# A pipelined attention kernel: near V in two transfers, regrouped Q/K stacks, a new setup and a new slot order

## What is computed

```python
OFFSETS = sorted(set(range(0, 33)) | {48, 64, 96, 128, 192, 256, 384})
qkv = x @ Wqkv + bqkv                      # q, k, v: 16 heads of 16
scores = [(q * shift(k, d)).sum(-1) * HD**-0.5 + pos_bias for d in OFFSETS]
alpha = softmax(scores)                    # over the offsets, d > position left out
out = sum(alpha[d] * shift(v, d) for d in OFFSETS)
x = layernorm(x + (out * sigmoid(x @ Wgate + bgate)) @ Wout + bout)
ids, probs = top2(relu(x @ rw1 + rb1) @ rw2 + rb2)
y = sum over the two experts of probs * expert(x), at most 1024 tokens an expert
out = layernorm(x + y)
```

## Time and profile before

| what | value |
|---|---|
| three runs, median | 1947.17 us (1945.5 to 1951.18) |
| the profiled execution: its own time, its span | 1936.55 us, 1934.8 us |
| mean granted TensorE clock | 0.761 of full speed |
| busy: TensorE, VectorE, ScalarE, GpSimd | 72%, 52%, 46%, 37% of the span |
| setup | to about 29 us |
| attention, 16 sequences | to about 1460 us |

### The profile page before, as it was taken

How to read it: one execution, slowest core, us unless ns; L and a number is a source line. 1 busy time by engine, 2 the same in 40 slices (tenths; PEclk the granted TensorE clock), 3 DMA queues, 4 the chain that set the end, 5 groups by cost and what they waited for, 6 DMA issues and landing times. The chain is left out here.

```text
span 1934.8 us, 72320 instructions
## 1 busy us (share of the span) xinstructions
PE 1400.3 (72%) x31232; PEld 893.4 (46%) x31232; DVE 1003.3 (52%) x2117; ACT 898.4 (46%) x1544; POOL 715.9 (37%) x654
## 2 busy tenths in 40 slices
PE   2345776877777786777777686877864599999970
PEld 1223444444444444444444444545542267666750
DVE  5214354655555555655655564655664355555425
ACT  3131462634454463635445363645453465566526
POOL 6021322624333352634434352634333122233235
PEclk9665676968676776867667686867676799999995
DMA  4483524436352434536252434535210534444328
GB/s 113 69 232 114 113 69 91 118 83 127 89 121 72 102 83 90 117 76 128 75 111 64 102 84 80 112 77 125 50 48 14 170 63 116 93 89 94 68 32 349
DMA packets 220104, 194.55 MB, mean 101 GB/s; under 512 B 66848, under 2 KB 207152, under 8 KB 219649
## 3 DMA queue, kind: packets, MB, share of 16 engines
q1 hardware_dynamic: 204464, 175.11, 36.5%
q0 software_dynamic: 15360, 15.10, 5.0%
HBM read 98.07 MB, written 86.18 MB: 95 GB/s over the span
## 5 line engine op out<-in xcount | busy, mean ns | idle before, releaser
L396 POOL TENSOR_TENSOR p<-p 128x512 f16<-128x512 f32 x96 | 129.5, 1349 | 357.8 <-ACT p L795 357.6
L809 ACT COPY featT<-gp 128x1024 f16<-128x1024 f16 x96 | 93.4, 1032 | 362.7 <-PE gp L541 362.7
L396 DVE TENSOR_TENSOR p<-p 128x512 f16<-128x512 f32 x96 | 85.5, 891 | 268.5 <-ACT p L795 268.2
L548 PE MATMUL gp<-featT,wr 128*128 128x512 f16 x768 | 191.5, 407 | 21.0 <-DVE mT L958 15.1
L1106 POOL DMA_INDIRECT disp<-y,sidx x128 | 180.1, 1407 | 53.2 <-issue 37.9
L1363 POOL DMA_INDIRECT xln<-y,place x64 | 104.9, 1640 | 217.5 <-DVE y L1505 176.2
L1401 PE MATMUL up<-rowsT,w 128*128 128x512 f16 x768 | 171.3, 383 | 8.7 <-DVE w L1478 5.3
L1415 PE MATMUL dn<-w,h 128*128 128x256 f16 x1536 | 170.1, 273 | 0.0
L1415 PEld LDWEIGHTS dn<-w,h 128*128 128x128 f16 x1536 | 149.7, 98 | 17.3
L794 ACT ACTIVATE p<-st 128x512 f16<-128x512 f32 x192 | 116.7, 608 | 77.9 <-PE st L592 75.1
L1462 ACT ACTIVATE h<-up,b 128x512 f16<-128x512 f32 x128 | 88.3, 690 | 128.7 <-PE up L1401 70.0
(11 more groups left out here) (174 smaller groups left out, 2881.7 us busy)
## 6 DMA issues: line engine op xcount, KB each, us to landing
qk_dram<-qk SPq DMA_DIRECT2D x64, 256.0 KB, 2.5
v_near<-vs SPq DMA_DIRECT2D x224, 66.0 KB
qs<-qk_dram SPq DMA_DIRECT2D x96, 128.0 KB, 4.4
ks<-qk_dram SPq DMA_DIRECT2D x96, 128.0 KB, 7.4
o_dram<-o_far SPq DMA_DIRECT2D x64, 136.0 KB, 7.3
o_back<-o_dram SPq DMA_DIRECT2D x16, 544.0 KB, 4.2
v_dram<-vs SPq DMA_DIRECT2D x16, 528.0 KB
v_far<-v_dram SPq DMA_DIRECT2D x64, 132.0 KB
```

Source lines behind the costliest of these rows:

```text
L396: engine.tensor_tensor(p16[:, b, 1, :], p32[:, b, :], p16[:, b, 0, :], ALU.subtract).then_inc(is_split, 1)
L548: last = nc.tensor.matmul(dst, lhs(a, c), rhs(b, c), start=(k == 0), stop=(k == len(todo) - 1))
L809: gp_done(nc.scalar.copy(featT[:, i, :, :].rearrange("f c t -> f (c t)"), bank[:, :].bitcast(F16)), n, stage, PART_OF_T[stage], i)
```

## The change

Q and K stacks: the columns of the weights and the bias are permuted in the setup so that channel d of the eight heads of one parity lie beside each other. A row of a stack is then one run of 8 KB in DRAM. SP stores the high halves as soon as ScalarE has them (`qk_hi`), reads rows 0 to 15 of each half with four DMAs of 128 KB (`hi_in`), then stores the low halves and reads the other 32 rows with four DMAs of 256 KB (`rest_in`). The maxima wait for the first, the scores for the second.

Near V: `v_near` is read from `v_dram`, which has 32 rows of zeros in front, by two DMAs of 64 rows. `vs` has one buffer. SP waits there, as before, until the near values of the sequence before are done.

Order: the gated transposes (`outp t`) go from slot 5 to slot 4, the first near scores from 4 to 5, the last near values from 15 to 16, the exponential of head half 0 of pair 0 from slot 0 to the slot before, and the subtraction `y` on VectorE two slots later.

Setup: x is loaded in it, `v_far` is cleared by ScalarE, `ks` by two whole memsets, and the first weights are split in smaller pieces. ScalarE issues six of the eight clearings of `disp` there and two at the end of iteration -1. SP regroups the bias through DRAM and writes the two pads of `v_dram`.

```diff
-    3: [("rank", "l"), ("proj", "vg1")], 4: [], 5: [("outp", "t"), ("rank", "c")],
+    3: [("rank", "l"), ("proj", "vg1")], 4: [("outp", "t")], 5: [("rank", "c")],
...
+         ("dve", "outp", "y"): 3,
...
-SCORES_AT = [-1, 0, 4, 7, 10, 12]
-EXP_AT = [0, 1, 5, 8, 11, 13]
+SCORES_AT = [-1, 0, 5, 7, 10, 12]
+EXP_AT = [[-1, 1, 5, 8, 11, 13], [0, 1, 5, 8, 11, 13]]
 SPLIT_AT = [1, 2, 6, 9, 12, 14]
-VALUES_AT = [2, 4, 7, 10, 13, 15]
+VALUES_AT = [2, 4, 7, 10, 13, 16]
...
-    v_dram = [dram(f"v_dram{i}", (N, H * VW), F16) for i in range(2)]
+    v_dram = [dram(f"v_dram{i}", (BLOCK + N, H * VW), F16) for i in range(2)]
...
-    qk_dram = [dram(f"qk_dram{i}", (4, D, N), F16) for i in range(2)]
+    qk_dram = [dram(f"qk_dram{i}", (2, 2, 2, P, N), F16) for i in range(2)]
...
-                if n.i is None and n.c == 0 and 1 <= h <= CLEARINGS:
-
-                    rows = slice((h - 1) * SLOTS // CLEARINGS, h * SLOTS // CLEARINGS)
-                    sync.dma_start(disp[rows, :].rearrange("(b p t) d -> p b (t d)", p=P, t=TILES),
...
                     wait(sp, pv_done, n.at(UNIT_PAIRS))
-                    sp.wait_ge(v_split, n.at(TILES, TILES))
+                    sp.wait_ge(v_stored, n.at(16, 16))
                     for u in range(2):
...
+                        half = PAIRS * VW
+                        src = bass.AP(v_dram[n.par].tensor, half * u, [[2 * half, 2 * BLOCK], [2 * half * BLOCK, N // BLOCK], [1, half]])
+                        dst = v_near[2 * BLOCK * u:2 * BLOCK * (u + 1), :, u, :, :]
+                        sync.dma_start(dst.rearrange("w b h c -> w b (h c)"), src).then_inc(v_near_in, 16)
...
-                sp.wait_ge(qk_split, n.at(4, 2 * w + 2))
                 if w == 0:
-                    wait(sp, stack_in[n.par], n.half(192))
...
+                    wait(sp, hi_in[n.par], n.half(64))
+                    wait(sp, rest_in[n.par], n.half(64))
+                sp.wait_ge(qk_hi, n.at(4, 2 * w + 2))
+                store(n, w, 0, qk_hi_stored)
                 if w == 0:
                     return
-                sp.wait_ge(qk_stored, n.at(64, 64))
                 for e in range(2):
                     wait(sp, st_full[e], n.at(UNIT_PAIRS, -UNIT_PAIRS))
...
+                sp.wait_ge(qk_hi_stored, n.at(32, 32))
+                for w, dst in ((0, qs), (1, ks)):
                     for e in range(2):
...
+                        src = qk_dram[n.par][w, e, PLACE[w][0]].rearrange("(d p) t -> d (p t)", p=PAIRS)
+                        sync.dma_start(dst[n.par][STACK * e:STACK * e + HD, :, :].rearrange("r p t -> r (p t)"), src).then_inc(hi_in[n.par], 16)
+                for w in range(2):
+                    sp.wait_ge(qk_split, n.at(4, 2 * w + 2))
+                    store(n, w, 1, qk_lo_stored)
+                sp.wait_ge(qk_lo_stored, n.at(32, 32))
+                for w, dst in ((0, qs), (1, ks)):
+                    for e in range(2):
+                        src = qk_dram[n.par][w, e].rearrange("i (d p) t -> (i d) (p t)", p=PAIRS)
+                        sync.dma_start(dst[n.par][STACK * e + HD:STACK * e + MROW, :, :].rearrange("r p t -> r (p t)"), src).then_inc(rest_in[n.par], 16)
...
-            load_x(Batch(None, 0))
+            for i in range(2):
+                sync.dma_start(v_dram[i][0:BLOCK, :], v_near_flat[0:BLOCK, 0:H * VW]).then_inc(pad_in, 16)
+            sp.wait_ge(pad_in, 32)
...
                 if k == 0:
+                    alone.wait_ge(rest_in[n.par], n.half(64, 64))
                     alone.wait_ge(m_in[n.par], n.half(32, 32))
...
-                    pe.wait_ge(stack_in[n.par], n.half(192, 192))
+                    pe.wait_ge(hi_in[n.par], n.half(64, 64))
...
-                        nc.scalar.activation(qk16[:, 0, u, :], bank[:, :], ACT.Identity, bias=bqk[:, u:u + 1], scale=scale)
+                        nc.scalar.activation(qk16[:, 0, u, :], bank[:, :], ACT.Identity, bias=bqk[:, u:u + 1], scale=scale).then_inc(qk_hi, 1)
...
+                if it.i is None and it.c == -1 and k == H - 1:
+
+                    act.wait_ge(rest_in[0], 64)
+                    for c in range(CLEARED_IN_SETUP, CLEARINGS):
+                        clear_slots(nc.scalar, disp, y16[0], c).then_inc(cleared, 16)
...
+                act.wait_ge(zeroed, 1)
+                for c in range(CLEARED_IN_SETUP):
+                    clear_slots(nc.scalar, g["disp"], zero_rows, c).then_inc(a["cleared"], 16)
+                wide = a["v_far_flat"][:, :].bitcast(FP32).rearrange("p (b c) -> p b c", c=704)
+                nc.scalar.copy(wide, zero_rows[:, :, :].rearrange("p t d -> p (t d)").bitcast(FP32)[:, 0:704].unsqueeze(1).to_broadcast([P, 6, 704]))
```

More of the change, by code:

```diff
@@ L202, in pair_at, with clear_slots @@
             return it.shift(-(at // H)), k
+def clear_slots(eng, disp, zero_rows, part):
+    rows = slice(part * SLOTS // CLEARINGS, (part + 1) * SLOTS // CLEARINGS)
+    return eng.dma_start(disp[rows, :].rearrange("(b p t) d -> p b (t d)", p=P, t=TILES),
+                         zero_rows[:, :, :].rearrange("p t d -> p (t d)").bitcast(U32).unsqueeze(1).to_broadcast([P, SLOTS // CLEARINGS // P // TILES, TILES * ROW // 2]))
 def tail(rows, dt):
@@ L290, in attention @@
         vg32 = sb("vg32", [P, 2, 2 * D], FP32)
-        vs = [sb(f"vs{i}", [P, TILES, H, VW], F16) for i in range(2)]
+        vs = sb("vs", [P, TILES, H, VW], F16)
         eg = [sb(f"eg{i}", [P, TILES * H, HD], FP32) for i in range(2)]
@@ L609, in values @@
                 if k == FAR_PAIRS:
-                    alone.wait_ge(v_near_in, n.at(256, 256))
+                    alone.wait_ge(v_near_in, n.at(32, 32))
                 p = lambda e, a, c: p16[:, 2 * (k % 2) + e, a, c:c + BLOCK]
@@ L1169, in _ @@
             def _(sp):
-                for k, (dst, src) in enumerate(loads):
-                    sp.dma_start(dst, src, allow_slow_non_contiguous=True).then_inc(here[k] if k < 6 else loaded, 16)
+                for k, (dst, src) in enumerate(loads[0:5]):
+                    sp.dma_start(dst, src, allow_slow_non_contiguous=True).then_inc(here[k], 16)
+                sp.dma_start(a["xin"][:, :, :], g["x_rows"][0:N, :].rearrange("(t p) d -> p t d", p=P)).then_inc(a["x_loaded"], 16)
+                sp.dma_start(*loads[5], allow_slow_non_contiguous=True).then_inc(here[5], 16)
+                for u in range(4):
+                    src = g["bqkv"][D * (u // 2):D * (u // 2 + 1)].rearrange("(p e d) -> e d p", e=2, d=HD)[u % 2]
+                    sp.dma_start(g["bqk_dram"][u].rearrange("(d p) -> d p", p=PAIRS), src, allow_slow_non_contiguous=True).then_inc(regrouped, 16)
+                for dst, src in loads[6:]:
+                    sp.dma_start(dst, src, allow_slow_non_contiguous=True).then_inc(loaded, 16)
+                sp.wait_ge(regrouped, 64)
+                sp.dma_start(a["bqk"][:, :], g["bqk_dram"].rearrange("u f -> f u"), allow_slow_non_contiguous=True).then_inc(loaded, 16)
                 sp.wait_ge(vec_done, 1)
@@ L1186, in _ @@
                     last = nc.gpsimd.memset(t[:, :], 1.0)
-                for i in range(2):
-                    last = nc.gpsimd.memset(a["vs"][i][:, :, :, HD:HD + 1], 1.0)
+                last = nc.gpsimd.memset(a["vs"][:, :, :, HD:HD + 1], 1.0)
                 last.then_inc(base, 1)
@@ L1227, in _ @@
                 for i in range(2):
-                    for e in range(2):
-                        nc.vector.memset(a["ks"][i][STACK * e + 32:STACK * (e + 1), :, :].bitcast(FP32), TWO_ONES)
+                    nc.vector.memset(a["ks"][i][:, :, :].rearrange("p a t -> p (a t)").bitcast(FP32), TWO_ONES)
                 for v in (vec_n[0], vec_f[0]):
@@ L1234, in _, with split @@
                 last.then_inc(vec_base, 1)
+                def split(k):
+                    src, h, l = splits[k]
+                    dve.wait_ge(hi, k + 1)
+                    nc.vector.scalar_tensor_tensor(l, src, WS, h, ALU.mult, ALU.subtract).then_inc(lo, 1)
+                for k in range(11):
+                    split(k)
                 dve.wait_ge(here[5], 16)
@@ L1244, in _ @@
                 last.then_inc(vec_done, 1)
-                for k, (src, h, l) in enumerate(splits):
-                    dve.wait_ge(hi, k + 1)
-                    nc.vector.scalar_tensor_tensor(l, src, WS, h, ALU.mult, ALU.subtract).then_inc(lo, 1)
+                for k in range(11, len(splits)):
+                    split(k)
 def experts(nc, g):
```

95 lines of the change are left out of this document (44 added, 51 removed).

## The result

The changed kernel takes 1864.92 us in the median of four runs (1862.24 to 1871.79), the kernel before 1946.34 us beside it: ratio 0.9608, 95% interval 0.9579 to 0.9637. The forecast was 1785, its range 1745 to 1860. So the sign was right, and half of the gain did not come: 81 us in place of 162.

| stretch | before | after | forecast | measured |
|---|---|---|---|---|
| start to the first mT | 83.9 | 90.5 | -16 | +6.6 |
| first to second mT (iteration 0) | 88.7 | 70.3 | -20 | -18.4 |
| second to last mT (14 periods) | 1197.9 | 1144.2 | -126 | -53.7 |
| last mT to the end of the span | 564.3 | 565.0 | 0 | +0.7 |

What follows compares the result with a forecast made beforehand. TensorE's start of near maximum 2 was taken as set by a chain: second far evacuation, store, landing, read back, merge, reduction. Periods 126, start 16 and iteration 0 20 sum to 162 us: 1774.6 profiled, 1785 median; range 1745 to 1860.

Steps and rivals of the forecast that it cites:

- Second far scores: Exponential of head half 0 moved earlier on ScalarE, so TensorE's wait for it goes: 2.84 us per period.
- High halves: Four stack reads instead of twelve ahead of near maximum 0: operands 13 us sooner, its wait goes entirely.
- Low halves and the rest: Low halves stored behind the first reads, then four 256 KB reads: done at 736.7, not holding the far sums.
- slow rest: Rival: 32-row stack reads go no faster than 16-row ones, done at 740.8; 5.4 us per period, 1835; chance 0.20.
- slower case: Rival: 8 KB runs on few rows make stack reads slower, sign under 90 GB/s; about 2050; chance 0.03.
- Gated transposes: Moved ahead of the first near scores on TensorE: 1.5 us to spare, no new wait; projection's 3.32 us wait goes.
- Late gate: Rival: gated low half on VectorE comes 4.5 us later, 3 lost per period: 42 us, 1827; chance 0.12.
- The chain: Far sums' store, o_back read and merge ahead of near maximum 2: 6.2 us sooner per period, still the next bound.
- Near V: Sixteen issues on SP become two from DRAM, its wait for the last near values covered: nothing added, nothing gained.
- The start: Ahead of the first near maximum: x loaded early 4.15 us, high halves 12 us sooner; sum 16 us.
- long setup: Rival: SP's small setup loads wait 15 us for the six clearings, first maximum gains 1 not 16; 1800; chance 0.10.
- Iteration 0: Clearings between transfers 14 us and an ordinary period's 9 go, less 3 for two clearings left: 20 us.

Runs made afterwards that it cites:

- old_order_y: Changed kernel with the slot tables of the kernel before, but the subtraction y kept at its new place two slots later; 1920.05 us, ratio 0.9894.
- old_order: Changed kernel with the slot tables of the kernel before, y early too; regrouped stacks, near V and new setup stay; 1938.31 us, ratio 0.9972.
- y_early: Changed kernel with only VectorE's subtraction y back at its old place, ahead of the reduction of near maximum 1; 1870.03 us, ratio 0.9634.

## Why the prediction was half right

- **Second far scores, 2.84 a period.** The wait went, but at the five turns it had covered the jump. That stop is now in the open, and longer. Here the step failed that the prediction put as "that exponential ends while TensorE is still at transposes and values. The wait goes": it let the time go with the wait. From mT to the next projection a period takes 24.0 us where 20.5 were forecast (23.4 before); with the loop written out it takes 20.6. Against `old_order_y` the new turn is worth 33 us, not 40, and the loop costs the changed kernel 15 to 30 us more than the kernel before.
- **High halves.** TensorE's row for the stacks is gone, as said. The words "that wait goes entirely" overlooked what is late next: VectorE, still at the ranking when it has to empty the output projection (22.8 us over the stretch).
- **Low halves and the rest.** Near, and harmless. The four reads are issued by 776.59 and the last lands at 781.34, 26.5 us behind the start of the projection; the forecast's 736.7 is 23.8 behind it and slow rest's 740.8 is 27.9. The far sums were ready at 777.96, so by the prediction's own sign slow rest came about. It costs nothing that shows: SP stores the far sums at 778.05 without waiting for that landing, and they have landed 4.7 us later (4.9 in the forecast). From first issue to last landing the 32-row reads moved 162 GB/s and the 16-row ones 88, a ratio of 1.84 for the prediction's 1.76. The slower case falls, though the 88 lies just under its sign of 90.
- **Gated transposes.** Right: no wait of TensorE at them for the gated low half, none for featT. Late gate falls.
- **The chain, 6.2 a period.** Its size was near: 5.5. But it does not stay the next bound: VectorE has merged o_back and waits for TensorE's near maximum 1 (789.50), which follows near maximum 0 and its wait for the ranking. And the prediction let TensorE go on from there without loss. From near maximum 3 to mT a period takes 21.4 us and not 20.4 (between the medians of the places), with issue rows where TensorE does many short products (L728, L609, L710). And y, costed as its own 1.49 us, was the gate behind o_back in the old order: where it stays, as in `old_order`, near maximum 2 is 2.0 sooner and no more. In the new order it is worth 5 us, within the noise (`y_early`).
- **Near V.** "Nothing added, nothing gained" holds in the changed kernel only because SP waits there for the last near values. With the old order the two transfers run at the turn beside x; that they lengthen the stop there is argued from one place in the trace, not shown alone.
- **The start, 16.** Wrong: the rival of the long setup came true, with 22 us. The rows of SP show the small loads held while ScalarE's clearings ran, on a queue of their own (21.66 us against 6.68). The Trainium skill (DMA: Bandwidth & Descriptors, "Issuing engines are not separate DMA queues") says that transfers share the DMA engines and interleave whichever engine issued them; these rows agree. The prediction named the rule and gave it 0.10.
- **Iteration 0, 20.** 18.4.

So two things failed: a bound that was named, given 0.10 and priced at 15 of its 22 us, and one that was not named, TensorE's supply of instructions. Of the 97 us between the forecast for a profiled execution, 1774.6, and the 1871.79 measured, 72 lie in the steady stretch and 23 ahead of the first mT. The issue rows stood in the view of the waits, 84 us of them in that stretch, and were read as fixed. The forecast of data waits was near (7.6 of 9.0 a period); the step from a wait to time was not.

## What to carry to other kernels

When a wait is removed, ask what the waiting engine does at once afterwards, its own supply of instructions included: rows of idle time that no semaphore explains, at runs of short instructions, can be a bound that grows when waits shrink. A loop's jump can lie hidden under a wait, as most of it did here at the turn of the kernel before, so a shorter critical path can make it dear; count the instruction loads and compare their ends with the ends of the stops. Large transfers that nobody waits for are not free in a setup whose tiny loads pass the same DMA engines: here they cost the first maximum 22 us.

## What the runs showed of the hardware

- TensorE runs out of instructions: stops without a releaser, mostly under 2 us at lines of short products and up to 5.8 at the turn, 12.0 us of an 82.7 us period. Those of more than 1 us (8.4 of the 12.0) end 1.2 to 2.5 us behind the end of a 16.4 KB load; that the shorter ones are waits for instructions too is inferred.
- A jump back of a loop costs instruction loads (9 more in an execution of the kernel before for five jumps, 14 in the changed one), and 0.7 or 5.3 us in the stretch where it stands, as there is a wait to hide it or not.
- Six clearings of 1 MB, issued by ScalarE on its own queue, held SP in issuing five loads of 4 KB for 21.66 us (6.68 without them).
